# Transposes in groups of two sequences, and an output block split by rank tiles, in a two-layer FFN kernel

## What is computed

```python
x = x + _L0_ffn_ref(_L0_cond_ref(x, ...), ...)
# second layer, condition: one weight matrix for each sequence b
c = einsum('bsi,oi->bso', x, W) + b
c = c + einsum('bsi,bio->bso', x, 2 * mask - 1) * coeff[:, None, None]
# second layer, experts: 64 of rank 16, the 16 best scores of each token
scores = c @ Wr.T
top_vals, top_idx = top_k(scores, 16)
G = zeros.at[rows, top_idx].set(softmax(top_vals))
h = einsum('nd,krd->nkr', c, A)
out = einsum('nkr,kdr->nd', h * G[:, :, None], B)
x = x + 2.0 * out
```

## Time and profile before

| | us |
|---|---|
| median of 3 runs | 355.6 |
| lowest and highest run | 355.43, 355.74 |
| profiled execution, its own time | 355.12 |
| its span in the trace | 353.4 |
| PE busy | 349.5 |
| DVE busy | 199.6 |
| ScalarE busy | 143.9 |
| GpSimd busy | 78.5 |

### The profile page before, as it was taken

How to read it: one execution, slowest core, us unless ns; L and a number is a source line. 1 busy time by engine, 2 the same in 40 slices (tenths; PEclk the granted TensorE clock), 3 DMA queues, 4 the chain that set the end, 5 groups by cost and what they waited for, 6 DMA issues and landing times.

```text
span 353.4 us, 4654 instructions
## 1 busy us (share of the span) xinstructions
PE 349.5 (99%) x1700; PEld 295.3 (84%) x1700; DVE 199.6 (56%) x301; ACT 143.9 (41%) x196; POOL 78.5 (22%) x86
## 2 busy tenths in 40 slices
PE   8999999999999999999999999999999999999996
PEld 7899888888888888888888898888888888888886
DVE  4786655334533453685674565869888867511101
ACT  5666544422442243545464471466352443200100
POOL 2560657863440004000000000000051145002200
DMA  6961343232120053397219019010051022201011
GB/s 223 325 204 43 114 134 116 79 104 75 54 79 0 0 178 125 85 391 291 61 32 305 6 37 416 24 58 5 0 179 60 0 61 60 59 32 59 32 59 59
DMA packets 14803, 37.32 MB, mean 106 GB/s; under 512 B 2273, under 2 KB 4225, under 8 KB 13505
## 3 DMA queue, kind: packets, MB, share of 16 engines
q1 hardware_dynamic: 11920, 31.21, 25.4%
q0 software_dynamic: 2432, 5.57, 5.3%
q10 hardware_dynamic: 432, 0.30, 0.3%
HBM read 34.97 MB, written 2.10 MB: 105 GB/s over the span
## 4 chain that ended last, share of the span: by engine, by line
PE 99%; DVE 0%; issue 0%
PE ps L1153 29%; PE ps L1155 29%; PE ps L1154 29%; PE ps L1175 3%; PE ps L1305 3%; PE ps L1395 1%; PE ps L1382 1%; PE ps L1190 1%; PE ps L1183 1%; PE ps L1194 1%; PE ps L1198 1%; PE ps L1230 1%; PE ps L1404 0%; PE ps L1413 0%; DVE x L1146 0%
## 5 line engine op out<-in xcount | busy, mean ns | idle before, releaser
L1153 PE MATMUL ps<-x_hl,w_hl 128*128 128x512 f32 x144 | 56.1, 390 | 0.0
L1154 PE MATMUL ps<-x_hl,w_hl 128*128 128x512 f32 x144 | 56.1, 390 | 0.0
L1155 PE MATMUL ps<-x_hl,w_hl 128*128 128x512 f32 x144 | 56.0, 389 | 0.0
L460 POOL TENSOR_TENSOR am_hl<-am_raw,am_hl 128x512 fp32r<-128x512 f32 x8 | 11.0, 1387 | 137.7 <-ACT am_hl L477 137.7
L416 POOL DMA_INDIRECT b_raw<-b_gu,row_of x32 | 32.0, 999 | 30.2 <-DVE b_st L778 22.2
L798 DVE TENSOR_TENSOR glu<-glu,ps 128x512 f32<-128x512 f32 (+1 forms) x22 | 14.9, 683 | 39.3 <-ACT glu L509 27.3
L1155 PEld LDWEIGHTS ps<-x_hl,w_hl 128*128 128x128 f32 x144 | 27.0, 188 | 5.7
L509 ACT ACTIVATE glu<-ps 128x512 f32<-128x512 f32 (+1 forms) x22 | 12.8, 589 | 46.3 <-PE ps L1175 46.1
L1153 PEld LDWEIGHTS ps<-x_hl,w_hl 128*128 128x128 f32 x144 | 27.1, 188 | 5.3
L1154 PEld LDWEIGHTS ps<-x_hl,w_hl 128*128 128x128 f32 x144 | 27.1, 188 | 5.2
L1153 PE MATMUL ps<-act,wd_hl 128*128 128x512 f32 x80 | 31.1, 389 | 0.0
(11 more groups left out here) (151 smaller groups left out, 730.8 us busy)
## 6 DMA issues: line engine op xcount, KB each, us to landing
wc_raw<-mask_w SPq DMA_DIRECT2D x8, 1024.0 KB, 7.3
w_raw<-w_gu SPq DMA_DIRECT2D x8, 512.0 KB, 3.2
wd_raw<-w_dn SPq DMA_DIRECT2D x10, 256.0 KB, 2.7
w_raw<-w_t SPq DMA_DIRECT2D x2, 1024.0 KB, 7.1
x<-x_t SPq DMA_DIRECT2D x2, 1024.0 KB, 6.1
am_raw<-a_moe SPq DMA_DIRECT2D x8, 256.0 KB, 2.6
bm_raw<-b_moe SPq DMA_DIRECT2D x4, 512.0 KB, 4.4
x_raw<-x_t SPq DMA_DIRECT2D x7, 256.0 KB, 4.5
```

The source lines that it names most:

```text
L460: nc.gpsimd.tensor_tensor(am_hl[:, j % AM_SLOTS, 1], am_raw[:, j % 2], am_hl[:, j % AM_SLOTS, 0].bitcast(F32), ALU.subtract).then_inc(am_l ...
L1153: nc.tensor.matmul(out, w_high, m_high, start=start, stop=False)
L1154: nc.tensor.matmul(out, w_high, m_low, start=False, stop=False)
L1155: return nc.tensor.matmul(out, w_low, m_high, start=False, stop=stop)
```

## The change

It consists of two parts. First, the transposes stand in groups of two sequences: turn(0) and turn(1) behind cond(2), turn(2) and turn(3) behind cond(4), turn(4) and turn(5) behind cond(6), turn(6) and turn(7) behind the first three matmuls of `experts(0)`. The copies `ct_high` on ScalarE and `ct_low` on DVE are put in an order that fits. Second, the last output block is made whole, in 18 matmuls of 512 columns, for the first six rank tiles, into bank 7, and DVE adds it; the last two rank tiles follow in two pieces of 256 tokens, 6 matmuls each, into banks 4 and 5, with an addition each. That is one addition more on DVE. The pieces' additions wait for the block's addition, and the two stores wait for counts of `late_banks_free` that are higher by one.

```diff
--- before.py
+++ after.py
@@ -70,6 +70,7 @@
 AM_SLOTS = 4
 H_ORDER = [(j + dj, s) for j in range(0, JT, AM_SLOTS) for s in range(2) for dj in range(AM_SLOTS)]
 HALF_TAIL = len(H_ORDER) - AM_SLOTS
+LAST_TILES = (JT - 2, JT - 1)
 
 
 def build(nc, x_t, small_in, mask_w, w_gu, w_dn, a_gu, a_dn, b_three, b_gu, b_dn,
@@ -381,7 +382,7 @@
                 sp.wait_ge(late_banks_free, 4 + n + 1)
                 half = slice(s * HALF, s * HALF + HALF)
                 sp.dma_start(out[o, :, half], x2[:, o, half]).then_inc(dma_out, 16)
-            sp.wait_ge(late_banks_free, 4 + 2 * KD + 1)
+            sp.wait_ge(late_banks_free, 4 + 2 * KD + 2)
             sp.dma_start(out[KD - 1, :, T - PAIR:T], x2[:, KD - 1, T - PAIR:T]).then_inc(dma_out, 16)
             sp.wait_ge(dma_out, 16 * 2 * KD)
             sp.wait_ge(dma_out_pair, 16)
@@ -729,7 +730,8 @@
             for b in range(BATCH):
                 if b + 2 < BATCH:
                     xs_high(b + 2)
-                if b:
+                if b and b % 2 == 0:
+                    ct_high(b - 2)
                     ct_high(b - 1)
                 if b + PREP < BATCH:
                     wc_high(b + PREP)
@@ -738,6 +740,7 @@
                     am_high(1)
                 if b == 5:
                     s_copy(0)
+            ct_high(BATCH - 2)
             ct_high(BATCH - 1)
             exponent(0)
             am_high(2)
@@ -768,7 +771,7 @@
                     bm_high((n - 8) // 2)
             for o in range(2, KD):
                 bm_high(o)
-            act_e.wait_ge(late_banks_free, 4 + 2 * KD)
+            act_e.wait_ge(late_banks_free, 4 + 2 * KD + 1)
             act_e.dma_start(out[KD - 1, :, HALF:T - PAIR], x2[:, KD - 1, HALF:T - PAIR]).then_inc(dma_out_pair, 16)
 
 
@@ -1087,17 +1090,24 @@
             wc_low(4)
             for b in range(BATCH):
                 c_bias(b)
+                if b == 4:
+                    ct_low(2)
+                    ct_low(3)
                 if b + 2 < BATCH:
                     xs_low(b + 2)
                 if b == 5:
                     wc_low_half(7, 0)
                     wc_low_half(7, 1)
-                if b:
-                    ct_low(b - 1)
+                if b == 2:
+                    ct_low(0)
+                    ct_low(1)
                 if 1 <= b < 5:
                     wc_low_half(5 + (b - 1) // 2, (b - 1) % 2)
                 if b == 6:
+                    ct_low(4)
                     route_first8(0)
+            ct_low(BATCH - 3)
+            ct_low(BATCH - 2)
             ct_low(BATCH - 1)
             route_next8()
             route_gates(0)
@@ -1134,7 +1144,7 @@
                 if n >= 5:
                     hg_low(n - 1)
             hg_low(2 * JT - 1)
-            for n in range(2 * KD - 1):
+            for n in range(2 * KD):
                 o, s = n // 2, n % 2
                 half = slice(s * HALF, s * HALF + HALF)
                 dve.wait_ge(o_ready, n + 1)
@@ -1142,8 +1152,9 @@
                     .then_inc(late_banks_free, 1)
             for h in range(2):
                 pair = slice(HALF + h * PAIR, HALF + h * PAIR + PAIR)
-                dve.wait_ge(o_ready, 2 * KD + h)
-                nc.vector.tensor_tensor(x2[:, KD - 1, pair], ps[:, 7 - 3 * h, 0:PAIR], x2[:, KD - 1, pair], ALU.add)\
+                dve.wait_ge(o_ready, 2 * KD + h + 1)
+                dve.wait_ge(late_banks_free, 4 + 2 * KD)
+                nc.vector.tensor_tensor(x2[:, KD - 1, pair], ps[:, 4 + h, 0:PAIR], x2[:, KD - 1, pair], ALU.add)\
                     .then_inc(late_banks_free, 1)
 
 
@@ -1431,11 +1442,14 @@
                 cond(b)
                 if b == 5:
                     scores(0)
-                turn(b - 1)
+                if b % 2 == 0:
+                    turn(b - 2)
+                    turn(b - 1)
                 if b == 6:
                     turn_scores(0)
             pe.wait_ge(c_done, BATCH - 1)
             experts(0, range(1))
+            turn(BATCH - 2)
             turn(BATCH - 1)
             experts(0, range(1, KD))
             scores(1)
@@ -1451,10 +1465,18 @@
             for n in range(6, 2 * JT):
                 experts(n)
 
-            def combine(o, u, s, bank, cols):
-                for j in range(JT):
-                    last = mm3(bank, bm_hl[:, u, 0, j], bm_hl[:, u, 1, j],
-                               hg[j // 2][:, j % 2, 0, cols], hg[j // 2][:, j % 2, 1, cols], j == 0, j == JT - 1)
+            def combine(o, u, s, tiles=range(JT)):
+                bank = ps[:, 4 + 2 * u + s]
+                for j in tiles:
+                    last = mm3(bank, bm_hl[:, u, 0, j], bm_hl[:, u, 1, j], hg[j // 2][:, j % 2, 0, halves(s)],
+                               hg[j // 2][:, j % 2, 1, halves(s)], j == 0, j == tiles[-1])
+                return last
+
+            def combine_pair(h):
+                cols = slice(HALF + h * PAIR, HALF + h * PAIR + PAIR)
+                for j in LAST_TILES:
+                    last = mm3(ps[:, 4 + h, 0:PAIR], bm_hl[:, 1, 0, j], bm_hl[:, 1, 1, j], hg[j // 2][:, j % 2, 0, cols],
+                               hg[j // 2][:, j % 2, 1, cols], j == LAST_TILES[0], j == LAST_TILES[-1])
                 last.then_inc(o_ready, 1)
 
             for o in range(KD):
@@ -1465,11 +1487,11 @@
                     pe.wait_ge(late_banks_free, 2 * o + s + 1)
                     pe.wait_ge(hg_lo, HALF_TAIL + AM_SLOTS * s)
                     if 2 * o + s < 2 * KD - 1:
-                        combine(o, u, s, ps[:, 4 + 2 * u + s], halves(s))
+                        combine(o, u, s).then_inc(o_ready, 1)
+            combine(KD - 1, 1, 1, range(LAST_TILES[0])).then_inc(o_ready, 1)
             for h in range(2):
-                if h == 1:
-                    pe.wait_ge(late_banks_free, 4 + 5)
-                combine(KD - 1, 1, 1, ps[:, 7 - 3 * h, 0:PAIR], slice(HALF + h * PAIR, HALF + h * PAIR + PAIR))
+                pe.wait_ge(late_banks_free, 4 + 4 + h + 1)
+                combine_pair(h)
 
 
 def constants():
```

## The result

The changed kernel takes 356.11 us (median of 15 runs, 355.82 to 357.3), the kernel before 355.43 beside it (15 runs, 355.0 to 355.82). The ratio is 1.0021 [1.0013, 1.0029]: slower, by 0.68 us as medians and 0.75 by the ratio, just at the 0.2% that was called the bound of what can be told. The forecast was 356.2.

What follows compares the result with a forecast made beforehand. PE was taken to bound the kernel, all of the chain but the last addition. +0.44 - 0.12 + 0.50 - 0.23 = +0.59 on a median of 355.6 gave 356.2 us, range 355.5 to 356.8.

Steps and rivals of the forecast that it cites:

- The first turn was a cover: Ahead of cond(2): without turn(0) there PE idles for the low features and pays turn(0) later, +0.44 (0.40 to 0.51).
- Groups saved: Conditioned stage on PE: fewer transpose groups save 0.05 each in the matmuls behind them, -0.12 (saving 0 to 0.2).
- turn(7) gets a new wait: Ahead of turn(7): PE waits for ct_low(5), now behind c_bias(7) on DVE, +0.50 (0 to 0.61).
- The condition under it: On DVE ahead of turn(7): the router block must have left by L + 0.43, when c_bias(7) starts; margin some 0.4.
- The first rival: On DVE: the router block overruns its margin, holds c_bias(7) and idles PE before turn(7); 0.8 to 1.3 slower, chance 0.17.
- The sentence against it: On DVE: the router block already ran its 2.31 beside two GpSimd operations, told against its holding c_bias(7).
- The last output block: End of PE's work: 18 matmuls of 512 and 12 of 256 columns replace 48 of 256, -0.23 (saving 0.2 to 0.25).
- The tail: Behind PE's last matmuls: DVE's added addition is hidden by 0.25, cost 0, bound above 0.2 for two stores in flight.
- Other waits and the clock: Conditioned stage: other moved waits stay covered; clock rival: half the granted clock adds 2.3 per ten matmuls, chance 0.02.
- The two rivals without one of the waits: Conditioned stage: turn(7) does not wait, +0.1, 355.7, chance 0.06; neither wait shows, -0.4, 355.2, chance 0.03.

Runs made afterwards that it cites:

- no-waits kernel: Changed kernel with turns 0 and 1 single, three more matmuls of experts(0) ahead of turn(6) and three of experts(1) ahead of scores(1): 355.5 us, ratio 0.9997 to before.
- GpSimd early: Changed kernel with ScalarE's copies am_high(0) and am_high(1) one sequence earlier, so GpSimd's pair runs earlier: 356.54 us (one run), +1.25 in the trace against before.
- `ct_low(5)` first: Changed kernel with ct_low(5) ahead of the router block on DVE, not behind c_bias(7): 356.86 us, ratio 1.0031 to the kernel before.
- the block alone: Kernel before with only the new last output block, transposes in single turns: 355.03 us, ratio 0.9982; again 354.98, ratio 0.9990.

## Why the prediction was right, step by step

- *The first turn was a cover: +0.44.* Exact: 0.43 lost ahead of cond(2), and 0.66 from cond(1)'s last matmul to cond(2)'s first with turn(0) or without. In the changed kernel DVE's end sets it: the low features end 0.10 ahead of cond(2).
- *Groups saved: -0.12.* From cond(2)'s second matmul to cond(7)'s last it was 21.03 before (237.39 to 258.42) and is 21.35 (237.87 to 259.22): +0.32, which is 0.44 - 0.12. The sum holds: two groups less in that stretch. The no-waits kernel gives 0.10 for three.
- *turn(7) gets a new wait: +0.50.* 0.57. With L at 259.22, `ct_low(5)` starts at L + 1.09, ends at L + 1.77 and PE resumes at L + 1.92; forecast were L + 1.04, 1.72 and 1.83. The condition under it failed: the router block was to leave DVE 0.4 ahead of `c_bias(7)`, and it left 0.05 too late (`c_bias(7)` started at L + 0.48), since its subtraction took 0.88 for 0.45. That is a count from these rows; in the one run meant to show it, GpSimd early, the block started late. The other 0.04 is PE, which resumed 0.15 behind `ct_low(5)` and not 0.11. The first rival was therefore there, with its cause, but the margin of 0.4 swallowed all but 0.05 of it. With `ct_low(5)` first the same rival decided, and its +1.18 lies inside the 0.8 to 1.3 it was given, though in another kernel. The sentence against it, that the block ran beside GpSimd already, was the weak one: it ran beside it in a harmless phase.
- *The last output block: -0.23.* -0.23 and -0.22 with this part alone. The distances were 0.227 and 0.120 again, as in the earlier trace rows. The rule that the prediction cites from the Trainium skill, page TensorE: Matmul & The Clock Gate, section Back-to-back issue gap, would have made this part worth 0.05, and these rows don't agree with it. That section states the rule for a single matmul by itself, not for a stream of weight loads and matmuls such as this one.
- *The tail: 0.* The last addition waited for PE by 0.21, forecast 0.25. The stores end as before.
- *Other waits and the clock.* No third wait; granted clock 1.00 with groups of eight transposes and both gaps.

The sum was +0.59; the anchored traces give +0.67, the difference being mostly turn(7)'s 0.07. That the median came within 0.09 of the 356.2 is in part luck: the forecast started from 355.6, the median of three runs, where fifteen gave 355.43, and this made up for the change's being 0.08 larger. The profiled execution, forecast at 355.7, took 356.27, since 0.47 were lost ahead of the changed places. The two rivals without one of the waits are out: both waits are in the rows.

## What to carry to other kernels

Before moving an instruction away because it costs 0.44, look at what the engine behind it would be waiting for: here a turn in front of a late operand was free, and was paid in full where it was moved to. When work is grouped, follow on the producing engine's queue the operation that frees the second buffer, for it may now stand behind a consumer's whole block. And a margin of a few tenths on DVE beside GpSimd is no margin until the DVE operations in between are checked for one that takes both inputs from SBUF: here the moment at which it met GpSimd's was worth up to 1.1 us (1.54 against 0.42).

## What was not expected of the hardware

One operation of DVE, `expo<-score,top` of 128x256, took 0.42 to 0.45, 0.88 or 1.54, by when it began during an operation of GpSimd: it ended 0.28 to 0.30 behind GpSimd's end in three kernels. GpSimd's second operation took 1.47 where DVE's had stood waiting for the first (before and after), and 1.29 where it came ahead of DVE's (`ct_low(5)` first). The `c_bias` and `ct_low` operations, which read one operand from PSUM, kept 0.68 to 0.69 where they overlapped with GpSimd's pair, by 0.2 to 0.3. The Trainium skill, page SBUF — State Buffer, section Who interferes with whom, states just this: a DVE instruction with two inputs in SBUF and a GpSimd instruction that reads SBUF block each other for a whole instruction, by order of arrival, while one with at most one input in SBUF does not. These rows agree, and the forecast, which priced such a delay from the 0.42 and 1.40 of the earlier trace rows without its cause, would have been sharper with it.

What stays open: whether grouped turns can beat single ones to the end. With no wait left they were 0.10 ahead up to the second turn of the scores, and 0.03 to 0.04 behind the block alone at the end of the trace, with 0.10 lost at the gates; by the medians of the runs they were 0.5 behind. A version that also gets the gates in time was not tried, nor another time for GpSimd's pair.
